# A gated cross-attention and mixture-of-experts block: the first loads put into another order

## The reference

```
h   = layernorm(x)
q   = qdq(h) @ qdq(wq).T + bq                 # qdq: rounded to int8 steps, row by row
k,v = split(ctx @ wkv.T + bkv)                # 8 x 1500 rows, 16 heads of 16
att = softmax(q k / 4) v
x   = x + tanh(g_xattn) * (qdq(att) @ qdq(wp).T + bp)
x   = x + tanh(g_ffn) * experts(layernorm(x)) # top 2 of 16, capacity 128, and a shared expert
```

## Time and profile before

| | us |
|---|---|
| median of 3 runs | 411.07 |
| the three runs | 410.23, 411.07, 413.10 |
| span of the profiled execution | 405.0 |

### The profile page before, as it was taken

One profiled execution on the slowest core, in us unless ns is written; L12 is line 12 of the kernel. 1 busy time (PEld: TensorE's weight loads), 2 busy tenths in 40 slices (PEclk: granted clock), 3 DMA queues, 4 the chain that ended last, 5 costly groups with the idle time before them and its releaser, 6 DMA issues.

```text
span 405.0 us, 14019 instructions
## 1 busy us (share of the span) xinstructions
PE 358.6 (89%) x5793; PEld 269.3 (67%) x5793; DVE 303.5 (75%) x656; ACT 250.9 (62%) x412; POOL 124.1 (31%) x116
## 2 busy tenths in 40 slices
PE   0896899999998998998999999998864699999993
PEld 0663468668677766855866776786643587888882
DVE  3888886775776676586577668668896877999993
ACT  3476477777686676776768666567721535666761
POOL 6151462132022122222203300001101054787870
PEclk9999699999999999999999999999985858999998
DMA  7869965565294186166336208544000009635001
GB/s 253 196 157 197 241 146 134 87 159 136 58 171 115 53 152 182 54 106 175 103 61 125 54 14 142 129 137 141 3 2 2 1 1 306 191 116 163 2 0 45
DMA packets 34512, 45.65 MB, mean 113 GB/s; under 512 B 3995, under 2 KB 30299, under 8 KB 34323
## 3 DMA queue, kind: packets, MB, share of 16 engines
q1 hardware_dynamic: 33395, 43.74, 44.5%
q0 software_dynamic: 640, 0.78, 0.9%
q10 hardware_dynamic: 416, 0.26, 0.3%
HBM read 25.08 MB, written 0.47 MB: 63 GB/s over the span
## 4 chain that ended last, share of the span: by engine, by line
PE 76%; DVE 13%; issue 5%; ACT 2%; POOL 2%; DMA 1%; DVEq 0%; ACTq 0%; POOLq 0%
PE PS L1035 35%; PE PS L1101 9%; PE PS L1078 8%; PE PS L1112 7%; PE PS L1363 4%; PE PS L1322 3%; DVE mx L794 2%; PE PS L1088 2%; PE PS L1346 2%; PE PS L1312 1%; DMA x_in<-x 1%; DVE KN L743 1%; PE PS L1279 1%; DVE st L697 1%; DVE mtop L798 1%
## 5 line engine op out<-in xcount | busy, mean ns | idle before, releaser
L794 DVE TENSOR_REDUCE mx<-PS 112x1 f32<-112x500 f32 (+1 forms) x128 | 114.3, 933 | 52.8 <-PE PS L1078 52.7
L501 ACT ACTIVATE PT_all<-PS 128x1344 f32<-128x1344 f32 x64 | 82.6, 1290 | 10.1 <-PE PS L1101 9.9
L1035 PE MATMUL PS<-cT,wkvT 128*128 128x500 f16 x288 | 71.5, 385 | 18.0 <-POOL slot_of L404 11.2
L1035 PE MATMUL PS<-wkvT,cT 128*125 128x256 f16 x576 | 73.2, 279 | 0.0
L1035 PEld LDWEIGHTS PS<-wkvT,cT 128*125 128x125 f16 x576 | 65.3, 139 | 5.3 <-issue 0.5
L395 POOL TENSOR_TENSOR cT<-c_in,cT 128x1000 f16<-128x1000 f32 x18 | 37.5, 2082 | 86.9 <-ACT cT L479 86.9
L1035 PEld LDWEIGHTS PS<-cT,wkvT 128*128 128x128 f16 x288 | 27.5, 99 | 50.8 <-POOL slot_of L404 11.2
L486 ACT ACTIVATE KN<-PS,col_in 128x500 f16<-128x500 f32 x48 | 32.5, 677 | 40.6 <-PE PS L1035 40.6
L1078 PE MATMUL PS<-arena,QC 96*112 96x500 f16 x192 | 52.4, 380 | 3.1 <-issue 2.8
L1101 PE MATMUL PS<-QC,arena 98*128 98x112 f16 x768 | 49.2, 214 | 3.0 <-ACT QC L521 2.9
L493 ACT ACTIVATE V<-PS 125x512 f32<-125x512 f32 x48 | 28.7, 598 | 30.6 <-PE PS L1035 30.6
(11 more groups left out here) (207 smaller groups left out, 463.8 us busy)
## 6 DMA issues: line engine op xcount, KB each, us to landing
arena<-KN SPq DMA_DIRECT2D x144, 125.0 KB, 3.6
c_in<-ctx SPq DMA_DIRECT2D x24, 500.0 KB, 4.5
cT<-W SPq DMA_DIRECT2D x11, 352.0 KB
c_in<-W SPq DMA_DIRECT2D x6, 352.0 KB
cT<-W SPq DMA_DIRECT2D x11, 176.0 KB
arena<-place_far SPq DMA_DIRECT2D x1, 1568.0 KB, 10.0
c_in<-W SPq DMA_DIRECT2D x6, 176.0 KB
PT_all<-L_xattn_wkv SPq DMA_DIRECT2D x1, 512.0 KB, 6.1
```

The costliest lines, as they stand in the source:

```text
L501: act.activation(PT_all[:, u % 4, :].rearrange("p (c k) -> p c k", c=CH), PS[:, 3:6, 0:4 * TP], ACT.Exp, scale=SCORE).then_inc(s["exp_done ...
L794: dve.tensor_reduce(mx[:, u % 2, k:k + 1], PS[0:TP, k:1 + k * (CH - 1), 0:CW], AX.XY, ALU.max).then_inc(s["red_done"], 1)
L1035: ins = mm(out_, w(a, h), x_(b, h), start=first and k == 0, stop=last and k == len(todo) - 1)
```

## The change

It changes the order of the first loads and of the work on them, and moves one subtraction to another engine.

- SP issues the keys' half of `wkv`, batch 0's first third, the values' half of `wkv`, x, the second third, `wq`, the last third, then `rows` and `gate`. ScalarE issues only `cols`. The semaphores are split to match.
- ScalarE rounds the keys' weights, the first context third, the values' weights, then the second third. VectorE makes the low halves in the order keys' weights, first third, values' weights; then x's statistics, the second third, `quantise_first`.
- TensorE waits for the keys' low half before the first key projection and for the values' before the first value projection.
- The tanh goes behind the high half of batch 1's last third; it has a semaphore of its own, for GpSimd.
- Batch 1's last low third is made by GpSimd, after the first query masks and ahead of the copies of the later queries; the counts of `tl_done` grow by one.

```
         def need_lo(eng, n, c):
-            if n < 2:
+            if n * CH + c < 2 * CH - 1:
                 need(eng, "tl0_done", n * CH + c + 1)
             else:
-                need(eng, "tl_done", (n - 2) * CH + c + 1)
+                need(eng, "tl_done", (n - 2) * CH + c + 2)
...
         def _(sp):
+            sp.dma_start(wkv_in[:, :, 0:D], wkv[:, :, 0:D]).then_inc(s["wk_loaded"], 16)
+            sp.dma_start(c_in[:, :, 0:CW], ctx_v[0, :, :, 0:CW]).then_inc(ctx_in[0], 16)
+            sp.dma_start(wkv_in[:, :, D:2 * D], wkv[:, :, D:2 * D]).then_inc(s["wv_loaded"], 16)
             sp.dma_start(x_in[:], ...).then_inc(s["x_loaded"], 16)
-            sp.dma_start(wkv_in, wkv).then_inc(s["wkv_loaded"], 16)
-            for c in range(CH):
-                ...
+            sp.dma_start(c_in[:, :, CW:2 * CW], ctx_v[0, :, :, CW:2 * CW]).then_inc(ctx_in[1], 16)
+            for k in range(NH):
+                sp.dma_start(wq_in[:, k, :], permuted(wq[k * 128:(k + 1) * 128, :])).then_inc(s["wq_loaded"], 16)
+            sp.dma_start(c_in[:, :, 2 * CW:M], ctx_v[0, :, :, 2 * CW:M]).then_inc(ctx_in[2], 16)
+            sp.dma_start(row_in[:], rows.partition_broadcast(TP), ...).then_inc(s["rows_loaded"], 16)
+            sp.dma_start(gateT[:], gate).then_inc(s["rows_loaded"], 16)
...
             for k in range(2):
                 gp.wait_ge(s[f"q_stacked{k}"], 16 * 3)
                 queries(0, k)
+            need(gp, "th_done", CH + 3)
+            gp.tensor_tensor(cT[:, 1, 1, :, 2 * CW:M], c_in[:, :, 2 * CW:M], cT[:, 1, 0, :, 2 * CW:M], ALU.subtract).then_inc(s["tl_done"], 1)
...
-            act.dma_start(row_in[:], rows.partition_broadcast(TP), ...).then_inc(s["small_loaded"], 16)
-            act.dma_start(gateT[:], gate).then_inc(s["small_loaded"], 16)
-            act.wait_ge(s["wkv_loaded"], 16)
-            ap.did(act.activation(wkvT[:, 0], wkv_in, ACT.Copy, scale=WS))
+            act.wait_ge(s["wk_loaded"], 16)
+            act.activation(wkvT[:, 0, :, 0:D], wkv_in[:, :, 0:D], ACT.Copy, scale=WS).then_inc(s["wkv_hi"], 1)
...
+            context_hi(0, 0)
+            act.wait_ge(s["wv_loaded"], 16)
+            act.activation(wkvT[:, 0, :, D:2 * D], wkv_in[:, :, D:2 * D], ACT.Copy, scale=WS).then_inc(s["wkv_hi"], 1)
+            act.wait_ge(s["cols_loaded"], 16)
             ap.did(act.activation(bk_c, bk_c, ACT.Copy, scale=WS))
-            context_hi(0, 0)
-            ap.did(act.activation(tg[:, 0:1], gx[:, 0:1], ACT.Tanh))
             context_hi(0, 1)
...
             context_hi(1, 2)
+            act.wait_ge(s["rows_loaded"], 32)
+            act.activation(tg[:, 0:1], gx[:, 0:1], ACT.Tanh).then_inc(s["tg_ready"], 1)
...
+            def weights_lo(k):
+                part = slice(k * D, (k + 1) * D)
+                dve.wait_ge(s["wkv_hi"], k + 1)
+                dve.scalar_tensor_tensor(wkvT[:, 1, :, part], wkv_in[:, :, part], WS, wkvT[:, 0, :, part], ALU.mult, ALU.subtract).then_inc(s["dve_pre"], 1)
+            weights_lo(0)
+            context_lo(0, 0)
+            weights_lo(1)
             dve.wait_ge(s["x_loaded"], 16)
             statistics(x_in, range(TT))
-            dve.wait_ge(s["act_pre"], 1)
-            dve.scalar_tensor_tensor(wkvT[:, 1], wkv_in, WS, wkvT[:, 0], ALU.mult, ALU.subtract).then_inc(s["dve_pre"], 1)
-            context_lo(0, 0)
+            context_lo(0, 1)
...
             quantise_first()
-            context_lo(0, 1)
             keys_lo(0, 0)
...
                 dve_slot(u)
-                if u == 0:
-                    context_lo(1, 2)
-                elif u == 1:
+                if u == 1:
...
             pe.wait_ge(s["dve_pre"], 1)
             project_keys(0, 0)
+            pe.wait_ge(s["dve_pre"], 2)
             project_values(0, 0)
```

More of the change, by code:

```diff
@@ L44 @@
 NCONST = 24
-NSMALL = 3 * 16
 ROWS = 2 * D + E + 2
@@ L243, in bank16 @@
             return PS[:, b, :].bitcast(F16)
-        names = """consts var_ready rstd_ready sp_ready x_loaded wq_loaded wp_loaded wkv_loaded small_loaded xq_ready xr_ready wqq_ready wpq_ready
+        names = """consts var_ready rstd_ready sp_ready x_loaded wq_loaded wp_loaded wk_loaded wv_loaded cols_loaded rows_loaded wkv_hi tg_ready xq_ready xr_ready wqq_ready wpq_ready
             sx_diag sp_diag pe_pre act_pre dve_pre qn_ready qb_done q_stacked0 q_stacked1 q_rest qp_read dve_step
@@ L290, in _ @@
         def _(sp):
+            sp.dma_start(wkv_in[:, :, 0:D], wkv[:, :, 0:D]).then_inc(s["wk_loaded"], 16)
+            sp.dma_start(c_in[:, :, 0:CW], ctx_v[0, :, :, 0:CW]).then_inc(ctx_in[0], 16)
+            sp.dma_start(wkv_in[:, :, D:2 * D], wkv[:, :, D:2 * D]).then_inc(s["wv_loaded"], 16)
             sp.dma_start(x_in[:], x.rearrange("b s d -> (b s) d").rearrange("(t p) d -> p t d", p=TP)).then_inc(s["x_loaded"], 16)
-            sp.dma_start(wkv_in, wkv).then_inc(s["wkv_loaded"], 16)
-            for c in range(CH):
[L295 to L298, removed]
+            sp.dma_start(c_in[:, :, CW:2 * CW], ctx_v[0, :, :, CW:2 * CW]).then_inc(ctx_in[1], 16)
+            for k in range(NH):
+                sp.dma_start(wq_in[:, k, :], permuted(wq[k * 128:(k + 1) * 128, :])).then_inc(s["wq_loaded"], 16)
+            sp.dma_start(c_in[:, :, 2 * CW:M], ctx_v[0, :, :, 2 * CW:M]).then_inc(ctx_in[2], 16)
+            sp.dma_start(row_in[:], rows.partition_broadcast(TP), allow_slow_non_contiguous=True).then_inc(s["rows_loaded"], 16)
+            sp.dma_start(gateT[:], gate).then_inc(s["rows_loaded"], 16)
             def load_context(n, c):
@@ L336, in load_weights @@
                 if j == 0:
-                    need(sp, "tl_done", CH * (B - 2))
+                    need(sp, "tl_done", CH * (B - 2) + 1)
                 if j == 2:
@@ L429, in _ @@
                     gp.dma_start(q16[PW * k:PW * k + PW, 4 * oh:4 * oh + 4, TP:T], qn[:, oh, k // 2, TP:T]).then_inc(s["q_rest"], 16)
-            gp.wait_ge(s["act_pre"], 3)
-            gp.wait_ge(s["small_loaded"], NSMALL)
+            gp.wait_ge(s["tg_ready"], 1)
+            gp.wait_ge(s["rows_loaded"], 32)
             gp.wait_ge(s["x_loaded"], 16)
@@ L466, in _ @@
             ap = Steps(act, s["act_pre"])
-            act.dma_start(col_in[:], cols).then_inc(s["small_loaded"], 16)
-            act.dma_start(row_in[:], rows.partition_broadcast(TP), allow_slow_non_contiguous=True).then_inc(s["small_loaded"], 16)
-            act.dma_start(gateT[:], gate).then_inc(s["small_loaded"], 16)
-            act.wait_ge(s["wkv_loaded"], 16)
-            ap.did(act.activation(wkvT[:, 0], wkv_in, ACT.Copy, scale=WS))
+            act.dma_start(col_in[:], cols).then_inc(s["cols_loaded"], 16)
+            act.wait_ge(s["wk_loaded"], 16)
+            act.activation(wkvT[:, 0, :, 0:D], wkv_in[:, :, 0:D], ACT.Copy, scale=WS).then_inc(s["wkv_hi"], 1)
             def context_hi(n, c):
@@ L562, in act_slot @@
                     w13_hi(0)
-            act.wait_ge(s["small_loaded"], NSMALL)
+            context_hi(0, 0)
+            act.wait_ge(s["wv_loaded"], 16)
+            act.activation(wkvT[:, 0, :, D:2 * D], wkv_in[:, :, D:2 * D], ACT.Copy, scale=WS).then_inc(s["wkv_hi"], 1)
+            act.wait_ge(s["cols_loaded"], 16)
             ap.did(act.activation(bk_c, bk_c, ACT.Copy, scale=WS))
-            context_hi(0, 0)
-            ap.did(act.activation(tg[:, 0:1], gx[:, 0:1], ACT.Tanh))
+            act.wait_ge(s["act_pre"], 1)
             context_hi(0, 1)
-            act.wait_ge(s["act_pre"], 2)
             keys_hi(0, 0)
@@ L771, in _ @@
             keys_lo(0, 1)
-            dve.wait_ge(s["small_loaded"], NSMALL)
-            dve.wait_ge(s["act_pre"], 5)
+            dve.wait_ge(s["cols_loaded"], 16)
+            dve.wait_ge(s["act_pre"], 3)
             dve.wait_ge(s["pe_pre"], 4)
@@ L784, in _ @@
             keys_lo(0, 4)
-            dve.wait_ge(s["act_pre"], 8)
+            dve.wait_ge(s["act_pre"], 6)
             dve.wait_ge(s["pe_pre"], 7)
@@ L1219, in _ @@
             pe.wait_ge(s["wqq_ready"], 1)
-            pe.wait_ge(s["act_pre"], 4)
+            pe.wait_ge(s["act_pre"], 2)
             for h in range(NH):
@@ L1225, in _ @@
             project_values(0, 2)
-            pe.wait_ge(s["act_pre"], 6)
+            pe.wait_ge(s["act_pre"], 4)
             project_queries(slice(0, TP), [PS[:, 2, k * TP:(k + 1) * TP] for k in range(NH)])
@@ L1236, in _ @@
             project_keys(0, 5)
-            pe.wait_ge(s["act_pre"], 7)
+            pe.wait_ge(s["act_pre"], 5)
             project_queries(slice(TP, T), [PS[:, 3 + 4 * k, 0:T - TP] for k in range(NH)])
             need(pe, "v_done", 5)
-            pe.wait_ge(s["act_pre"], 8)
+            pe.wait_ge(s["act_pre"], 6)
             pe.wait_ge(s["qp_read"], 2 * NH)
```

## The result

The change made the kernel slower, by 0.8%. Over 20 runs each the medians are 413.47 us after (409.48 to 418.40) and 410.15 before (406.56 to 413.78); the ratio is 1.0077, with a 95% interval of 1.0052 to 1.0101. The forecast was 0.7% faster, 408.3, with a range from 404.8 to 412.0. The profiled execution after took 411.47 for a span of 409.7, against a span of 405.0 before, so the profiles differ by 4.7 us; a single profile carries a scatter of a few microseconds that the ratios average out.

What follows compares the result with a forecast made beforehand. Up to 56 us VectorE's work and its waits beside GpSimd were taken to hold TensorE, afterwards TensorE itself. Gains of 0.3 (first stretch) and 2.5 (second) make 2.8: 411.07 - 2.8 = 408.3 us, range 404.8 to 412.0.

Steps and rivals of the forecast that it cites:

- The early start: First stretch: TensorE's first projection near 8.0 instead of 11.20, 3.2 us earlier, of which 0.3 remains by Wq.
- Turns at rstd: Before the normalisation: VectorE's second low third and GpSimd's rstd run one after the other, 2.4 us instead of 1.2.
- The preamble wait: First token tile's quantisation on VectorE beside GpSimd's DMA issues, memsets and iotas: 0.6 us, bounds 0 and 1.5.
- rival 2: TensorE's idling before 19.3 us lowers its clock for 6.5 us, losing 3.2: 411.5 us; chance 0.20.
- The wait at the moved third: Before slot 0: VectorE's own low third waits 1.38 us for GpSimd's, moving the first reduce to 37.4.
- The second stretch to slot 3: Slots 0 to 3: key projection done before the second reduce, third reduce 1.3 us earlier; 2.5 gained at 56.18.
- The next slot meets the burst with a wait of 1.2: Second stretch: maxima avoid the 2.04 us stall beside GpSimd's burst once; the following slot waits 1.2 us.

Runs made afterwards that it cites:

- e2: Changed kernel with GpSimd's bias scaling and its addition to x moved to batch 5; ratio to the kernel before 1.0048.
- e6: Changed kernel with query halves in a tile of their own and maxima steps with one SBUF tensor each; ratio to the kernel before 1.0007.
- e11: Changed kernel with only batch 2's second and last thirds held back on SP; ratio to the kernel before 1.0110.
- e1: Changed kernel with GpSimd's late constants and DMA issues ahead of its wait for the variance; ratio to the kernel before 1.0036.
- e3: Changed kernel with the small maxima steps written with one SBUF tensor and a per-partition scalar; ratio to the kernel before 1.0100.
- e12: Kernel before with only batch 1's last low third moved to GpSimd, loads and weights as they were; ratio to the kernel before 1.0003.
- e4: Changed kernel with batch 1's last low third back on VectorE, so new load order and split weights alone; ratio to the kernel before 1.0049.
- e7: Changed kernel with own query tile, one-input maxima and GpSimd's late constants ahead of the variance wait; ratio to the kernel before 0.9998.
- e9: As e7, with batch 2's second and last thirds also held back on SP; ratio to the kernel before 0.9932.
- e10: Kernel before with own query tile, one-input maxima and batch 2's second and last thirds held back; ratio to the kernel before 0.9897, median 404.54 us.

## Why the prediction was wrong

- **The early start: right, and worth nothing.** TensorE began at 8.01 (8.0). ScalarE began the first third at 5.59 (5.6); x and the second third were later than I summed, 9.08 against 8.1 and 10.35 against 9.5. The first reduce comes at 35.3 to 40.6 us in the ten profiles with the new order, at 34.9 to 36.1 in the four with the old one, so the 3.2 us bought nothing there even where no stall was.
- **Turns at rstd: wrong.** Rows L391 and L719 after show both at full speed together (L719 took 1.20 in all ten kernels with the new order), so about 1 us that I charged was not paid. A rule of the Trainium skill (SBUF — State Buffer, "Who interferes with whom"), that a VectorE instruction with two SBUF inputs contends with a GpSimd instruction that reads SBUF, did not bear out for this rstd on 112x4 elements; it did for L719 beside L428 and for the maxima.
- **The preamble wait: mis-sized, 2.2 for 0.6.** I held that short instructions would block briefly. The normalisation lost 2.2 us across several of them, more than the 1.5 of my upper bound. The rule that I set aside, of the same page of the Trainium skill and the same section, is that a tensor_scalar in a two-port mode blocks; the trace agrees in that the instruction was held (2.61 against 0.41), but no row shows its mode. All seven profiles with this order on GpSimd (after, e2 to e6 and e11) have the wait: 2.1 to 2.2 us in four, about 1.0 in the three where the normalisation got through and the scaling was held. Why it got through there stays open. With the wait VectorE was through with Wq, by the mark of the earlier trace rows, at 20.35, not 19.3, and rival 2's fall of the clock followed, 0.50 from 19 to 22, about half as long as I priced it. The fall does not hang on the stall alone: e11 has the stall and 1.00 from 18 to 22, e1 has no stall and 0.64.
- **The wait at the moved third: right.** L719 beside L428 waited 1.26 (1.38).
- **The second stretch to slot 3: right in mechanism.** The projection ran at 1.43, the turned scores came at 44.16 without a low third to wait for, and from the second query product to the fourth reduce the change won 3.6 us (1.15 + 2.48). Its maxima fell ahead of GpSimd's burst.
- **"The next slot meets the burst with a wait of 1.2": the step that failed.** The wait was 5.5 us (5.63 - 0.16), and TensorE came out of it at the lower clock: 6.7 us lost within two slots (-2.48 to +4.18). I priced the stall by the end of one GpSimd instruction, as the earlier trace rows show. With GpSimd's last low third no longer waiting for ScalarE, there was no gap until 57.18, and VectorE waited through four. e3 removed it by changing only the form of the maxima; e2 and e12 show that whichever slot comes early meets the same run. In e12 it takes the whole gain of the moved third (1.0003); the new order of the loads, which the changed kernel has besides, then leaves it slower (1.0077, and 1.0049 alone in e4).
- **Not in the prediction at all:** the slots that come earlier outrun the transfers. I charged the transfers of the second stretch with nothing. Already in the changed kernel the third exponential waits 4.01 us for the query copies, hidden beside the 5.5. e3, e6 and e7 have the fifth reduce 3.8 to 5.8 us earlier than before and give it back to the query copies (e3) and to TensorE's "issue"; e9 and e10 show that it is the loads issued too soon.

The mechanism that I gave the forecast was there and even larger, but it moved TensorE into two limits whose size did not depend on it. With the maxima, the tile and the loads all seen to, the change itself brings nothing that can be measured: the intervals of e9 (0.9932) and e10 (0.9897) overlap. Two things remain open. One is why VectorE gets in between two GpSimd instructions at one place and not at the next: it did at 51.16 in the kernel before and, at the same place of GpSimd's stream, behind the addition of the bias (L436, L439), in the one after (L808, 0.28), but at none of the three places that follow. The other is whether TensorE's "issue" is the instruction block itself, which no run held by itself.

## What to carry to other kernels

A stall of one engine beside another is bounded by the whole run of back-to-back instructions on the other engine, not by one of them; so look how long that engine goes on without an idle gap, and write small steps in the form that was not held here, with one SBUF tensor. Work that is made earlier reaches the next limits earlier too: before costing a gain, list what the earlier slots will find unfinished (copies, loads, instructions), and hold back loads that nobody needs yet. When one limit is removed and the time stays, look again for "issue" and for the same instruction grown long: here three edits together gave up to 1%, none of them alone on the changed kernel gave a gain clear of the intervals, and whether two would do with the loads held was not run.

## What the runs showed of the hardware that was not expected

- A VectorE instruction of 0.16 us was held 5.63 us by consecutive GpSimd instructions, within a hundredth the same in six kernels (5.62 or 5.63); the same work with one SBUF tensor took 0.22 beside them.
- A tensor_scalar on 112x256 was held 1.0 to 2.2 us beside DMA issues, memsets and iotas of GpSimd, in all seven kernels that have them there; in three of these the first such instruction got through and a later one was held.
- rstd on GpSimd (1.04) and a low third on VectorE (1.20) ran together without loss.
- With the transfer engines full, copies of queries issued by 48.3 us freed their tile only at 57.2 in the changed kernel, and in e7 TensorE stood 5.07 us with no semaphore to wait for.
